# First image pair split by image, and VectorE's reads of the product banks reordered

## The reference

```python
out = lax.conv_general_dilated(x, weight, window_strides=(1,), padding=[(4, 4)],
                               dimension_numbers=('NCH', 'OIH', 'NCH'), feature_group_count=4)
ctx = jnp.einsum('nd,od->no', c, c_weight)
y = out + ctx[:, :, None] + bias[None, :, None]
w = kernel.astype(x.dtype) * 2.0 - 1.0          # kernel: booleans, 1024 x 1024
return x + scale * jnp.einsum('bsi,if->bsf', y, w)
```

## Time and profile before

| | |
|---|---|
| median of 3 runs | 169.41 us (167.74 to 169.68) |
| time of the profiled execution | 169.69 us |
| its span, first to last instruction | 167.8 us |
| TensorE busy, matmuls | 160.5 us (96%), 918 |
| VectorE busy | 137.3 us (82%) |
| ScalarE busy | 71.9 us (43%) |
| GpSimd busy | 42.8 us (25%) |
| TensorE clock granted | 1.000 of full speed throughout |

### The profile page before, as it was taken

The page is one execution under the profiler, slowest core; times in us unless marked ns, Lnnn a source line. Parts: engine busy times, 40 slices in busy tenths (PEclk is TensorE's granted clock), DMA queues, the critical chain, the costliest instruction groups (busy, mean ns, idle before and its releaser), DMA issues.

```text
span 167.8 us, 2771 instructions
## 1 busy us (share of the span) xinstructions
PE 160.5 (96%) x918; PEld 135.8 (81%) x918; DVE 137.3 (82%) x180; ACT 71.9 (43%) x65; POOL 42.8 (25%) x49
## 2 busy tenths in 40 slices
PE   7999999999997979999999999999999999999992
PEld 2579889898985859887898889887998879888782
DVE  4926749979899999779996899779977999779944
ACT  3336693453872047520791169223772071204200
POOL 5622850005300604007310334015400612000000
PEclk9999999999999999999999999999999999999999
DMA  5889499977879969898968989897988782806014
GB/s 199 256 190 326 119 206 197 236 108 191 187 222 239 215 129 399 211 238 194 251 201 224 259 154 344 191 244 161 297 221 232 110 280 53 197 4 250 0 79 171
DMA packets 27101, 33.51 MB, mean 200 GB/s; under 512 B 3568, under 2 KB 19376, under 8 KB 27088
## 3 DMA queue, kind: packets, MB, share of 16 engines
q1 hardware_dynamic: 21600, 25.36, 56.1%
q10 hardware_dynamic: 4912, 6.78, 15.2%
q0 software_dynamic: 576, 1.20, 3.7%
HBM read 10.19 MB, written 8.40 MB: 111 GB/s over the span
## 4 chain that ended last, share of the span: by engine, by line
PE 33%; DMA 18%; SPq 17%; DVE 12%; ACTq 8%; issue 6%; ACT 4%; DVEq 0%
SPq L240 16%; DMA x_nat<-x 10%; PE ps_conv L821 9%; ACTq L482 8%; PE ps_A L865 8%; DMA y_sum<-y_two 6%; DVE sums L642 5%; PE ps_C L865 4%; ACT x_phase L460 3%; PE ps_conv L846 3%; DVE x_nat L663 3%; PE ps_A L881 2%; PE ps_B L881 2%; PE ps_C L881 2%; DMA x_blk<-x_phase 2%
## 5 line engine op out<-in xcount | busy, mean ns | idle before, releaser
L422 POOL TENSOR_TENSOR set<-x_blk 128x512 f32<-128x512 f32 x12 | 17.4, 1470 | 63.8 <-DMA x_blk<-x_phase 63.8
L503 ACT CAST hi<-sums 128x1024 fp32r<-128x1024 f32 x14 | 14.7, 1050 | 41.7 <-DVE sums L642 35.8
L663 DVE SCALAR_TENSOR_TENSOR x_nat<-ps_A,scale_col,x_nat 128x512 f32<-128x512 f32 x27 | 20.2, 748 | 13.1 <-PE ps_A L865 12.3
L460 ACT COPY x_phase<-x_nat 128x1032 f32<-128x1032 f32 x13 | 27.3, 2144 | 3.9 <-issue 2.7
L865 PE MATMUL ps_A<-sign_T,hi 128*128 128x512 f32 x80 | 22.1, 398 | 1.0 <-issue 1.0
L503 ACT CAST hi<-y_sum 128x1024 fp32r<-128x1024 f32 (+1 forms) x14 | 11.7, 832 | 25.9 <-DMA y_sum<-y_two 20.1
L865 PE MATMUL ps_A<-sign_T,lo 128*128 128x512 f32 x80 | 21.5, 391 | 0.0
L422 POOL TENSOR_TENSOR w_bytes<-x_blk 128x512 f32<-128x512 f32 x12 | 12.3, 1048 | 23.0 <-DVE sums L642 19.0
L865 PEld LDWEIGHTS ps_A<-sign_T,lo 128*128 128x128 f32 x80 | 14.9, 188 | 3.5 <-DVE lo L652 0.4
L865 PEld LDWEIGHTS ps_A<-sign_T,hi 128*128 128x128 f32 x80 | 14.5, 188 | 4.0 <-issue 1.4
L846 PEld LDWEIGHTS ps_conv<-toeplitz,set 128*128 128x128 f32 x144 | 17.0, 192 | 0.5
(11 more groups left out here) (109 smaller groups left out, 237.9 us busy)
## 6 DMA issues: line engine op xcount, KB each, us to landing
x_nat<-x SPq DMA_DIRECT2D x16, 512.0 KB, 4.4
out<-x_nat SPq DMA_DIRECT2D x15, 512.0 KB, 4.9
x_blk<-x_phase SPq DMA_DIRECT2D x114, 64.5 KB, 3.1
y_sum<-y_two ACTq DMA_DIRECT2D x48, 128.0 KB, 3.3
w_bytes<-w_bool SPq DMA_DIRECT2D x2, 512.0 KB, 5.9
x_blk<-x_phase POOLq DMA_DIRECT2D x8, 64.5 KB, 3.2
shift<-shift_dram POOLq DMA_DIRECT2D x2, 256.0 KB, 7.2
x_blk<-x_phase ACTq DMA_DIRECT2D x6, 64.5 KB, 4.1
```

The costliest lines, as they stand in the source:

```text
L422: nc.gpsimd.tensor_tensor(dif[r][:, e], x_blk[r][:, :, e:e + M:2], x_blk[r][:, :, e + 1:e + 1 + M:2][:, :, 0:K], ALU.subtract).then_inc(di ...
L460: nc.scalar.copy(x_phase[r][:, :, 0:M + 1], line(d, r, 0, PAD + L + PAD).rearrange("r (m q) -> r q m", q=B)).then_inc(phase_ok[r], B)
L503: nc.scalar.copy(parts(hi_all, k), group(k)).then_inc(hi_ok[k], 1)
L663: nc.vector.scalar_tensor_tensor(there, bank[b], scale2_col[:, :], there, ALU.mult, ALU.add).then_inc(summed[k], 1)
```

## The change

At the start pair 0 is loaded as two transfers of 64 rows, one for each image. VectorE brings image 0 to phases as soon as it is there (`x_image[0]`) and ScalarE image 1. SyncE issues all four blocks of image 0, and block 6; ScalarE 7, GpSimd 4 and 5. Pair 1's blocks are shared out as before. TensorE takes pair 0's blocks in the order 0, 1, 2, 3, 7, 6, 4, 5.

In the plain product of double 0 the last two products change places (bank E done ahead of C); VectorE's read of E moves to where that of C was, and that of C into step 1. T4, a sum of signs that P4 needs, is made in two halves; the first half moves from step 1 to ahead of the last shift of double 1. In the later steps C21_A comes ahead of S2, S4 ahead of the low part of S1 and S2, C11_P1 ahead of C11_P2, and C11_P2 behind the first pair's `fast_y`; in step 1 it comes behind C22_A. GpSimd's second pair waits for that low part in place of S4.

```diff
-FIRST_BLOCKS = {("ACT", 0): (2, 3), ("SP", 0): (0, 1), ("POOL", 1): (4, 5), ("SP", 1): (6,), ("ACT", 1): (7,)}
-FIRST_ORDER = (2, 0, 3, 1), (4, 6, 5, 7)
+FIRST_BLOCKS = ({"SP": (0, 1, 2, 3, 6), "ACT": (7,), "POOL": (4, 5)},
+                {"SP": (0, 1, 6), "ACT": (2, 3, 7), "POOL": (4, 5)})
+FIRST_ORDER = ((0, 1, 2, 3), (7, 6, 4, 5)), ((2, 0, 3, 1), (4, 6, 5, 7))
...
-            eng.wait_ge(phase_ok[r], B)
-            for h in range(2):
-                for a in FIRST_BLOCKS.get((of, h), ()):
-                    to_block(eng, r, a, blk_first[r][a])
+            for a in FIRST_BLOCKS[r][of]:
+                if r == 0:
+                    eng.wait_ge(phase_first[a // GROUPS], 1)
+                else:
+                    eng.wait_ge(phase_ok[1], B)
+                to_block(eng, r, a, blk_first[r][a])
...
-        def first_phases(copy, q):
-            return copy(x_phase[0][:, q, 0:M + 1], x_nat[:, 0, :].rearrange("r (m q) -> r q m", q=B)[:, q])
+        def first_phases(copy, i):
+            rows = slice(i * C, (i + 1) * C)
+            return copy(x_phase[0][rows, :, 0:M + 1], x_nat[rows, 0, :].rearrange("r (m q) -> r q m", q=B))
...
-            load(0, 0, x_first[0])
+            for i in range(2):
+                rows = slice(i * C, (i + 1) * C)
+                sp.dma_start(x_nat[rows, 0, PAD:PAD + L], x_pairs[0][rows]).then_inc(x_image[i], 16)
...
-                    pool.wait_ge(s_ok["S4"], d - 1)
+                    pool.wait_ge(lo_ok["S12"], d - 1)
...
             def step(d):
                 if d > 1:
-                    sum_up("C21_A", d - 1)
                     combine("S3", d)
+                    combine("S4", d)
                     low_part("S12", d)
-                    combine("S4", d)
-                if d > 1:
-                    sum_up("C11_P2", d)
                     sum_up("C11_P1", d)
                 if runs(d, 2):
                     fast_y(d + 1, 0)
                 if d == 1:
+                    sum_up("C11_P1", d)
+                    plain_sum("C")
+                else:
                     sum_up("C11_P2", d)
-                    sum_up("C11_P1", d)
                 low_part("A22", d)
...
-                if d == 1:
-                    plain_sum("E")
-                    last_signs(slice(0, KH // 2))
...
                     low_part("A", d + 1)
                     combine("S1", d + 1)
                     sum_up("C12_C", d)
+                    sum_up("C21_A", d)
                     combine("S2", d + 1)
```

44 lines of the change are left out of this document (24 added, 20 removed).

## The result

| | before | after |
|---|---|---|
| median | 169.55 us (6 runs) | 172.25 us (6 runs) |
| profiled execution | 169.69 us | 172.02 us |
| its span | 167.8 us | 170.0 us |
| TensorE's first convolution matmul | 8.67 | 9.38 |
| first plain product | 17.05 | 18.58 |

The ratio of the two is 1.0142, 95% interval 1.0083 to 1.0201: the change costs time, and whether the loss reaches 2% is open. The medians lie 2.7 us apart, the two profiled executions 2.33. The forecast was 170.7, and its range held the time; but three of its four terms were off, as the trace shows stage by stage.

The account below looks back on a forecast made before the run. The prediction took TensorE to bound the kernel. From the profiled 169.69 us it summed 0 for the start, -1.7 for step 1, +2.0 for steps 2 to 5 and +0.7 for the last step to 170.7, range 167.3 to 172.8.

Parts of the forecast that it names:

- The start: Pair 0's loads, copies and blocks up to the first convolution matmul: taken as 0, between +0.6 and -0.4 us.
- (b): At the start: a block leaving earlier lands no earlier, behind SyncE's sign bytes; best case 0.4 us gained.
- (c): At the start: SyncE sends four blocks in sequence, ScalarE copies image 1, blocks 4 to 7 leave later; worst 0.6 lost.
- rival 2: At the start: 64-row half loads are slow, image 1 comes later; 0.4 to 1.0 over forecast, 171.4 middle, chance 0.25.
- signs of being wrong: Trace marks against the forecast, among them image 1 over 1 us behind image 0, first matmul below 8.3 or above 9.2.
- rival 1: The forecast itself: in the steps the wait changes place; 170.7 us, own range 169.5 to 171.9, chance 0.35.
- Step 1: P7's wait goes, P1 starts at 59.0, convolution at 61.8 and not 63.52: 1.7 of 2.9 us gained.
- Steps 2 to 5: The wait for C21_A becomes one for ScalarE's odd columns, 18.8 us a step, plus one collision: 2.0 us lost.
- the collision with GpSimd: In steps 2 to 5: GpSimd's subtraction starts before VectorE's low part and delays it; 0.6 us, counted once in four steps.
- Rival 3: In steps 2 to 5: GpSimd first every time, four collisions and not one; 172.6 us, chance 0.12.
- The last step: The read behind P2, now behind that of P1, delays the read P3 waits for: 0.7 us lost.
- Rival 5: Whole kernel: the reordering works throughout, 4.3 us come back, 0.7 go in the last step; 165.9 us, chance 0.10.

Follow-up runs that it names:

- half_loads: Kernel before, with only pair 0's load cut in two transfers of 64 rows, both awaited by both copies; 170.99 us, ratio 1.011.
- column_loads: Kernel before, with the first pair loaded as two transfers of 128 rows and half the columns each; 169.88 us, ratio 1.006.
- start_whole_load: The changed kernel's start with one whole load of the first pair, VectorE's order as before; 169.55 us, ratio 0.9986.
- reads_only: Kernel before with only the change's order of VectorE's reads, start as before; 170.69 us, ratio 1.0108.
- p4_behind_s2: reads_only with the read C21_A put back behind S2; 170.91 us, ratio 1.0121.
- Combined: reads_only with ScalarE's odd columns made ahead of high S12 and C11_P2 moved twice; 167.64 us, ratio 0.9926.
- odd_early: Kernel before, with only ScalarE's odd columns of the next step's first pair made ahead of high S12; 169.05 us, ratio 1.0001.
- after_odd_early: The changed kernel, with only ScalarE's odd columns of the next first pair made ahead of high S12; 169.22 us, ratio 0.9992.
- start_only: Kernel before with only the change's loads, copies and blocks of pair 0, VectorE's order as before; 171.4 us, ratio 1.0082.
- combined_last: Combined, with C21_A behind S2 ahead of the last step alone; 166.14 us, ratio 0.9823.

## Why the prediction was right, and where not

**The start: predicted 0, between +0.6 and -0.4; measured +1.5.** This step failed. Its part (b), that the first block is behind the sign bytes whatever one does, held, though not its 8.4: the sign bytes landed at 8.6 and block 0 at 8.97. Its part (c) counted ScalarE's longer copy for the blocks behind it alone, "blocks 4 to 7 leave 1.2 later than now", and left out the Toeplitz copy that stands in the same queue; that is the 0.71 at the first matmul. (In the two other profiles of this start it was VectorE's Toeplitz copy, behind the late pair 1.) Its reason for taking 0, that blocks of this time land in order of their issue, doesn't hold: blocks 7 and 4, issued at 8.06 and 8.33, landed at 12.33 and about 11.4. And the load of image 1 at 5.90 was not in the term but in rival 2, which had named its condition (64 rows at half the rate), its sign ("image 1 landing over 1 us behind image 0": 1.54) and a price of 0.4 to 1.0. The price was too small, as it ended at the first block; the stop at block 7 came on top, 0.8 by the plain product's mark (1.53 later) less the 0.71. Rival 2 held, with 0.25 against 0.35 for the forecast. Two of the signs of being wrong came with it: image 1 over 1 us behind image 0, and the first matmul above 9.2 (9.38). The median of 172.25 also lies above rival 1's own range of 169.5 to 171.9. Half_loads, column_loads and start_whole_load show the slow landing by itself.

**Step 1: predicted 1.7 gained; 1.02 in the profiled executions.** P7's wait went, and with it the low part's 1.95. P1 was forecast at 59.0; it came at 61.17, which is 59.7 when the start's 1.48 is taken off. Most of the 0.7 between them is S1's wait for `y_sum`. That transfer was nowhere in the term. P1 still waits 0.26 for C21_A there, where the prediction's sign of being right was no such wait. But the table shows this step between 18.07 and 23.79 with no edit in it that explains 5 us, so a difference of 1 us between two profiled executions is no measure of the change, and the gain of step 1 stays unproven in either size.

**Steps 2 to 5: predicted 2.0 lost; 0.92 measured.** The mechanism was right: "the wait for C21_A becomes a wait for the odd columns", with periods of 18.72 where 18.8 was forecast, in all steps but one. Reads_only has it in all four, 1.2 lost. Against the mean of the five kernels with the old order the two losses are 1.1 and 1.4, so the 0.92 is partly the draw of before's one profile; and the prediction's own 4 x 18.8 is 75.2, a loss of 1.5 and not 1.4. The rest of the 2.0 was the collision with GpSimd, 0.6, which did not come in the changed kernel: ScalarE's phases did start 1.27 behind the convolution, as the 1.3 of the estimate, but GpSimd began 12.35 to 13.2 behind it, not 11.5 to 12.3. That was near, and partly luck: in reads_only GpSimd began at 11.82 once, 0.03 behind the low part, and in p4_behind_s2 at 11.32, ahead of it, in a step of 18.90. Rival 3 (four collisions) came in no run.

**The last step: predicted 0.7 lost; 0.73 measured.** The size is right, but the reason given is half of it. The prediction blamed the read behind P2. Combined undid that and kept 22.43. Each of two reorderings is enough for the same 0.6 there, and only with both undone does it go away.

**Rival 5** (all of it works, 165.9) needed "S2 not to matter", and S2 mattered. With ScalarE's order mended it came within reach: 166.1.

The sum was 170.7, the changed kernel's profiled execution 172.02. The start's 1.5 too little and step 1's 0.7 too much gain make 2.2; steps 2 to 5 at 1.1 too much loss take half of it back; the 0.2 that are left lie outside the marks. So the forecast came near by a share of luck: errors of both signs were in it.

## What to carry to other kernels

Where a wait is short, look for the second one that ends almost at the same time: here 0.21 us for a read and 0.40 us for a copy hid each other, neither edit alone gave anything, and both, with the rest of the reordering, gave 0.8 to 1.4%. A reordering that puts a read ahead of a sum moves everything that hangs on the sum, on other engines too, and turns a wait that the sum had filled into idle time. And a transfer cut by partitions was not two transfers at half the time each. Cut by columns the halves landed sooner, but the kernel still lost 0.6%; left whole, with two engines copying a half each, it lost nothing.

## What the runs showed beyond that

**A stop costs more than the trace's idle time.** The odd_early step with a listed idle of 0.21 takes 18.56 against 18.07: 0.49. The first four matmuls behind the stop take 1.17 and not 1.07, and the idle time counts from the modelled end of the matmuls before, where back to back they overlap by 0.16 (a product half starts every 0.91 and lasts 1.07). The wait of 0.40 for the odd columns makes a step of 18.73, 0.66 longer. So a wait of this kernel counts as its idle time and some 0.27 more.

**Late first blocks can cost TensorE's clock.** In half_loads the copies came so late that TensorE stood still for 0.83 us ahead of the Toeplitz matrix and 0.74 ahead of the first convolution matmul, at 11.10. Its granted clock by stretches (window, then busy time and count of PE, PEld, DVE, ACT, POOL, clock, DMA share, GB/s):

```profile
8.00:10.00 2.00, 1.92 (x20) 1.26 (x17) 1.28 (x3) 0.12 (x1) 0.88 (x2) 0.95 0.81 208
10.00:12.00 2.00, 1.26 (x5) 0.93 (x4) 0.86 (x4) 0.47 (x1) 1.05 (x2) 0.50 0.87 208
...
16.00:18.00 2.00, 2.00 (x12) 1.44 (x12) 0.69 (x2) 0.30 (x1) 1.22 (x1) 0.84 0.84 305
```

```profile
12.58 3.78 PE L823 MATMUL ps_conv<-toeplitz,x_blk 128*128 128x128 f32 x16
```

The clock stood at its lower level, 1.2 GHz, from 10 to about 16 us, and 16 matmuls took 3.78 us where they take 2.05 in column_loads. After_odd_early, which stood still for 1.34 us ahead of its first convolution matmul at 10.82, had the same (0.50 from 10.5 to about 20 us), with its plain product at 23.67, 5 us behind that of the changed kernel with the same start. Start_only stood still for 1.46 us ahead of its first matmul at 10.37 and kept the full clock, so the length of that stop alone doesn't tell. The granted clock of each run, taken over the whole execution, says how often it came: 0.97 or 0.98, as in these two profiles, in 2 of start_only's 12 runs, 1 of after_odd_early's 12 and 1 of half_loads' 5, and in none of the changed kernel's 6 or of the 73 listed runs of the kernel before. So the new start brings the kernel near a second, larger loss in some of its executions.

**Step 1 depends on landings.** Stops of 1.2 to 2.3 us for the second pair's odd columns, which wait for its blocks (47.26 in odd_early, 48.76 in start_whole_load), or of 0.3 to 1.6 at P1, behind S1's wait for `y_sum` (61.17 in the changed kernel, 64.09 in combined_last), come and go. The longest, 2.34 us in start_whole_load, was followed by the lower clock too, 0.50 from 50 to 52 us, where 24 matmuls took 4.54 us and not 2.9; that is in its 23.79. Step 1 is the largest source of spread between the profiles here, and it was not in the prediction. What makes a transfer late there stays open.
